# Norm shifts moved from GpSimd to VectorE, C rows asked for three places behind B rows, and a rewritten order table

## The chip, the cores and the metric

The kernel runs on one core of one Trainium2 chip. TensorE (PE), VectorE (DVE), ScalarE (ACT) and GpSimd (POOL) each run their own instruction list in order and wait for each other by semaphores. SyncE (SP) issues most of the transfers. The metric is device time of one launch, in microseconds. The kernel before took 2023.14 us in the median of three runs (2008.57, 2023.14 and 3804.73 us).

## The reference

Eight sequences of 512 tokens with 256 features go through four layers: an attention without a softmax over the score matrix (layer 0), two state-space layers (1 and 2, the second on permuted tokens), and another attention (layer 3). Every layer starts with a norm over the features, and the attentions have a second norm behind their products. Cut to what matters here:

```python
xn = (x - mean) * rsqrt(var + 1e-5)                        # "norm": root = rsqrt, shift = -mean * root
# state-space layer: 512 channels, 16 states each
xz = modulated(xn) @ W_in;  u = silu(conv4(xz[:512]));  z = xz[512:]
dt_r, B, C = split(u @ W_x, [64, 80]);  dt = softplus(dt_r @ W_dt + b_dt)
for t in range(512):                                       # h: [512 channels, 16 states]
    h = h * exp(dt[t, :, None] * A) + (dt[t] * u[t])[:, None] * B[t]
    y[t] = h @ C[t]
out = x + gate * (((y + u * D) * silu(z)) @ W_out)
```

## The kernel before

A **scan** is one state-space layer of one sequence; there are 16 of them. Channels lie on the 128 partitions in 4 chunks, tokens on the free axis. One **unit** is the recurrence of one chunk and one of the 16 states over all 512 tokens: one scan instruction of VectorE (lines 1578 and 1581). A scan has 64 units, the program 1024. Two units that follow each other share a state number, so that they share a row of B and a row of C: there are 512 such pairs, called rows below.

For a pair the work goes like this. SP asks for the row of B and the row of C from DRAM, spread over the partitions (lines 893 and 897; each has 4 slots). The **injection** is `dt*u*B`: for pairs of one kind ("beside", 224 of them) POOL makes it in the state buffer (line 960), for the others ("spread", 288) ACT copies the row of B into a PSUM bank (line 1292) and VectorE multiplies there (line 1571). ACT makes the decay `exp(dt*A)`, in a PSUM bank (line 1284) or in SBUF (line 1303). VectorE scans. Then the **weight**, the state times C, is made by POOL in place (line 969; VectorE does the last two pairs), and PE adds the weighted states up in PSUM (line 2016), which frees the state buffer. There are 14 state buffers of one unit each.

Beside the units run chains of other work: 16 attentions, and for every scan a prep (norm, projections, convolution), a tail and a post. Each is a generator with named stages. A norm that ACT makes is: sums, squares, `root` (Ln and Exp, lines 1015 and 1017), then POOL's **shift** (line 919, 128 x 4 elements, one instruction), then four `normed` activations on ACT that read the shift (line 1042). Five attention norms and one prep norm are made by VectorE instead; their `normed` (line 1428) doesn't read the shift, but the shift is still made, since its semaphore counts norms. There are 48 shifts: 32 of attentions and 16 of preps.

What sets the order: nothing at run time. `run_batches` walks through all units in quarter-unit steps, and each engine, building its own list, issues in each step what the tables say: `STEPS` (how many quarter units before or behind its scan an injection, a row copy, a decay, a weight or a sum stands), `GATES`, `SKIPS`, and the `*_STAGES` tables with the step of each stage of each chain. So the tables are the order of all engines' lists, and a wait at the head of a list holds all that stands behind it. 1024 units are 4096 quarter units.

SP's list, per scan, is: ask for B of row g as soon as its slot is free (`used`), then for C of row g-1 as soon as POOL's weight of the row four before it is done (`past(sp, m_prod, ...)`), then B of row g+1, and so on.

Of the kernel before, what the change touches and what calls it, by code (L numbers as in the profile page):

```python
# [17 lines left out]
HALVES = 2  # L18
# [12 lines left out]
TAIL_BASE, POST_BASE, PREP_BASE = -19, -50, 8  # L31
ATT_BASES, LATE_BASES = (18, 100, 153, 222), (41, 193)
# [11 lines left out]
LATE_PAIRS = 2  # L44
PIECES = 3
# [32 lines left out]
def by_name(names, durations):  # L78
# [146 lines left out]
         225),  # L225
})
TAIL_STAGES = by_name(TAIL_NAMES, {
    0: (104, 105, 106, 106, 109),
    1: (2, 68, 72, 73, 75),
    2: (61, 75, 78, 86, 91),  # L230
    3: (59, 73, 77, 85, 91),
# [1882 lines left out]
```

## Time and profile before

| | |
|---|---|
| runs | 2008.57, 2023.14, 3804.73 us |
| the profiled execution | 2021.5 us, span 2019.3 us |
| granted TensorE clock, mean of the span | 0.961 |
| busy, of the span | PE 90%, DVE 88%, ACT 85% (1710.2 us), POOL 89% |
| first and last work of POOL on a scan | 108.15 us, 1957 us |
| first and last scan instruction of VectorE | 113.56 us, 1957.84 us |

The busy shares alone don't separate the engines: four are near 90% of the span. The span has three parts: 108 us in which the weights and masks are loaded and the first attentions and the first prep run, 1849.7 us from POOL's first instruction for a scan to VectorE's last scan, and 61.5 us for the last post and the last attention, which run one behind the other.

### The profile page before, as it was taken

The page shows a single profiled execution, that of the slowest core. Times are in us where ns is not written, and L with a number is a line of the kernel's source. Part 1 is how long each engine was busy: PE and PEld are TensorE (multiplying, and loading weights), DVE is VectorE, ACT ScalarE, POOL GpSimd, SP SyncE. Part 2 cuts the span into 40 slices and gives each one's busy share as a digit, 9 for nine tenths or more (in the row PEclk, how much of TensorE's full clock was granted, in tenths as well). Part 3 has the DMA queues.
Part 4 walks back from the last instruction along what each step waited for, and adds up shares of the span by engine and source line. Part 5 has one row for each costly group of instructions (what it writes and reads, how often), then busy time and mean ns, then how long its engine had stood idle before and what let it go on. Part 6 is the DMA issues. An engine that isn't in the chain of part 4 may idle for free. (4 is left out here: it accounts for less than half of the span.)

```text
span 2019.3 us, 29111 instructions
## 1 busy us (share of the span) xinstructions
PE 1817.7 (90%) x9252; PEld 1265.7 (63%) x9252; DVE 1780.9 (88%) x1818; ACT 1710.2 (85%) x3224; POOL 1789.5 (89%) x823
## 2 busy tenths in 40 slices
PE   8979688998989999998999999898998999697778
PEld 7555555757667575766667575656757575455666
DVE  5458999889999999999989999999989999898983
ACT  2488788989989999999989999999989998777662
POOL 0059999999999999999999999999999999999970
PEclk8989699999999999999999999999999999898999
DMA  7034554444445545454444545445444545454430
GB/s 279 1 110 156 169 165 149 139 159 155 150 140 171 167 146 181 130 182 153 146 150 152 178 149 175 147 157 162 157 140 155 166 154 180 142 162 142 155 105 11
DMA packets 163784, 302.29 MB, mean 150 GB/s; under 512 B 18904, under 2 KB 27312, under 8 KB 162096
## 3 DMA queue, kind: packets, MB, share of 16 engines
q1 hardware_dynamic: 153110, 287.45, 43.9%
q10 hardware_dynamic: 10522, 12.99, 2.1%
q8 instruction: 74, 1.21, 0.2%
q14 instruction: 78, 0.64, 0.1%
HBM read 292.98 MB, written 5.29 MB: 148 GB/s over the span
## 5 line engine op out<-in xcount | busy, mean ns | idle before, releaser
L969 POOL TENSOR_TENSOR state<-state,c_rows 128x1024 f32<-128x1024 f32 x510 | 1197.2, 2382 | 26.3 <-DVE state L1578 13.6
L1581 DVE TENSOR_TENSOR_SCAN state<-decay,mix_banks 128x512 f32<-128x512 f32 x576 | 673.1, 1206 | 15.7 <-ACT decay L1303 0.7
L2016 PE MATMUL bank<-const_sb,state 128*128 128x128 f32 x4096 | 546.4, 281 | 38.1 <-POOL state L969 37.7
L2016 PEld LDWEIGHTS bank<-const_sb,state 128*128 128x128 f32 x4096 | 482.1, 145 | 145.9 <-issue 76.4
L1578 DVE TENSOR_TENSOR_SCAN state<-mix_banks,state 128x512 f32<-128x512 f32 x448 | 525.4, 1204 | 48.0 <-ACT mix_banks L1284 36.4
L960 POOL TENSOR_TENSOR state<-kept,b_rows 128x1024 f32<-128x1024 f32 x224 | 532.4, 2381 | 19.7 <-DMA b_rows<-flat_rows 10.3
L1303 ACT ACTIVATE decay<-kept,ssm_pack 128x512 f32<-128x512 f32 x576 | 395.2, 716 | 17.0 <-DVE state L1581 14.2
L1571 DVE TENSOR_TENSOR mix_banks<-kept,mix_banks 128x1024 f32<-128x1024 f32 x288 | 353.5, 1227 | 42.4 <-ACT mix_banks L1292 33.6
L1284 ACT ACTIVATE mix_banks<-kept,ssm_pack 128x512 f32<-128x512 f32 x448 | 302.0, 683 | 57.4 <-DVE state L1581 42.2
L1836 PE MATMUL bank<-kept,conv_diag 128*128 128x512 f32 x496 | 225.3, 597 | 4.3 <-ACT kept L1224 3.8
L987 ACT ACT_TABLE_LOAD x165 | 211.7, 1283 | 8.8 <-issue 5.8
L1698 PE MATMUL bank<-att_pack,xnT 128*128 128x256 f32 x704 | 187.5, 409 | 0.0
L1292 ACT ACTIVATE mix_banks<-b_rows 128x512 f32<-128x512 f32 x288 | 169.2, 589 | 21.4 <-DVE state L1578 16.9
L1698 PEld LDWEIGHTS bank<-att_pack,xnT 128*128 128x128 f32 x704 | 131.0, 197 | 38.3 <-issue 23.3
L1836 PEld LDWEIGHTS bank<-kept,conv_diag 128*128 128x128 f32 x496 | 90.8, 191 | 97.4 <-issue 90.6
L935 POOL TENSOR_TENSOR kept<-kept 128x1024 f32<-128x1024 f32 x32 | 76.1, 2378 | 53.1 <-ACT kept L1161 49.7
L1825 PE MATMUL bank<-ssm_pack,kept 128*128 128x512 f32 x256 | 117.6, 596 | 3.9 <-ACT kept L1215 1.9
L1815 PE MATMUL bank<-kept,ssm_pack 128*128 128x512 f32 x256 | 118.0, 597 | 0.7 <-ACT kept L1203 0.4
L1905 PE MATMUL bank<-gated_w,kept 128*128 128x256 f32 x480 | 108.0, 381 | 2.6 <-ACT kept L1268 2.4
L1905 PEld LDWEIGHTS bank<-gated_w,kept 128*128 128x128 f32 x480 | 89.5, 190 | 16.4 <-issue 5.0
L919 POOL TENSOR_TENSOR att_shift<-att_minus,att_rstd 128x4 f32<-128x4 f32 x32 | 6.7, 209 | 98.5 <-ACT att_rstd L1017 98.5
L1677 PE MATMUL bank<-const_sb,xn 128*128 128x128 f32 x352 | 56.9, 286 | 26.9 <-ACT xnT L1144 10.5
(206 smaller groups left out, 2237.9 us busy)
## 6 DMA issues: line engine op xcount, KB each, us to landing
b_rows<-flat_rows SPq DMA_DIRECT2D x512, 256.0 KB, 3.9
c_rows<-flat_rows SPq DMA_DIRECT2D x512, 256.0 KB, 3.6
conv_diag<-conv_diag SPq DMA_DIRECT2D x8, 1024.0 KB, 7.3
out<-x_res ACTq DMA_DIRECT2D x8, 512.0 KB, 3.2
ssm_pack<-ssm_pack SPq DMA_DIRECT2D x2, 1907.0 KB, 12.4
x_next<-x ACTq DMA_DIRECT2D x6, 512.0 KB, 6.7
x_again<-x_dbl ACTq DMA_DIRECT2D x16, 128.0 KB, 4.3
state<-ada_w SPq DMA_DIRECT2D x1, 1536.0 KB, 14.3
```

The costliest lines, as they stand in the source:

```text
L960: pool.tensor_tensor(pair_states(g), dtu[:, c:c + HC], by_pair(b_rows[:, row % ROWS]), ALU.mult).then_inc(m_inject[BESIDE], 1)
L969: pool.tensor_tensor(st, st, by_pair(c_rows[:, row % ROWS]), ALU.mult).then_inc(m_prod, 1)
L987: act.preload_act_table_set(name)
L1284: act.activation(mix_banks[BANK_OF[g]], dt[:, c, :], ACT.Exp, scale=neg_a[scan_of(si)[0]][:, c * N + n:c * N + n + 1]).then_inc(m_decay[BE ...
L1303: act.activation(decay[:, nth(g) % DECAYS, :], dt[:, c, :], ACT.Exp, scale=neg_a[scan_of(si)[0]][:, c * N + n:c * N + n + 1]).then_inc(m_d ...
L1571: dve.tensor_tensor(both, dtu[:, c:c + HC, :], by_pair(mix_banks[row]), ALU.mult).then_inc(m_inject[SPREAD], 1)
L1578: ins = dve.tensor_tensor_scan(st, mixed, st, 0.0, ALU.mult, ALU.add)
L1581: ins = dve.tensor_tensor_scan(st, decay[:, nth(g) % DECAYS], mixed, 0.0, ALU.mult, ALU.add)
L1698: ins = pe.matmul(dst, lhs[:, c, t * P:(t + 1) * P], weights[:, c, :], start=False, stop=(t % 2 == 1 and c == DC - 1))
L1836: ins = pe.matmul(dst[:, late:], conv_diag[:, c * TAPS + TAPS - 1 - late, :], u[s][:, c, 0:T - late], start=(late == 0), stop=(late == TAP ...
L1905: ins = pe.matmul(dst[:, (t % 2) * D:(t % 2 + 1) * D], lhs[:, c, t * P:(t + 1) * P], weights[:, c, :], start=(c == 0), stop=(c == CH - 1))
L2016: ins = pe.matmul(y_banks[c2][:, t * P:(t + 1) * P], state[:, g % STATES, t * P:(t + 1) * P], ident, start=False, stop=(g == BANK_SUMS[g / ...
```

## The change

Three things change. The shift goes from POOL's list to VectorE's, with the same operands and the same semaphores (for norms that VectorE makes itself, it stands ahead of `normed`). C rows are asked for three places behind their B rows, not one. And all tables of the order are new: the two that place POOL's work stand, in the mean, at 13.0 quarter units behind the scan for a weight (12.0 before) and 16.8 ahead of it for an injection (15.2 before); the sums stand 24.9 behind (24.5 before).

```diff
-TAIL_BASE, POST_BASE, PREP_BASE = -19, -50, 8
-ATT_BASES, LATE_BASES = (18, 100, 153, 222), (41, 193)
+TAIL_BASE, POST_BASE, PREP_BASE = -17, -46, 9
+ATT_BASES, LATE_BASES = (18, 100, 152, 221), (41, 193)
...
+C_BEHIND = 3
...
 STEPS = {
-    "weight": (11, 7, 10, 5, 9, 8, 6, 8, 9, 14, 14, 11, 15, 13, 12, 8, 7, 8, 12, 7, 5, 8, 6, 12, 11, 19, 17, 14,
...
+    "weight": (9, 5, 8, 8, 9, 8, 6, 15, 11, 10, 10, 14, 13, 9, 9, 6, 7, 7, 10, 6, 7, 8, 6, 16, 13, 13, 13, 10, 9,
...
-                for g in range(HALVES * N + 1):
+                for g in range(HALVES * N + C_BEHIND):
...
-                    if g > 0:
-                        slot, n = (g - 1) % ROWS, (g - 1) % N
-                        past(sp, m_prod, si * HALVES * N + g - ROWS)
+                    if g >= C_BEHIND:
+                        g -= C_BEHIND
+                        slot, n = g % ROWS, g % N
+                        past(sp, m_prod, si * HALVES * N + g + 1 - ROWS)
                         sp.dma_start(c_rows[:, slot, :], flat_rows[parity, N + n].partition_broadcast(P)).then_inc(c_loaded[slot], 16)
...
-            def shift(norm, root, done, k):
-                pool.wait_ge(root, k)
-                pool.tensor_tensor(norm["shift"][:, :, 0], norm["minus"][:, :, 0], norm["rstd"][:, :, 0],
-                                   ALU.mult).then_inc(done, 1)
...
             def attention(ai, layer, s, b):
-                w = Walk(ATT_STAGES[ai])
-                yield from w.to("root")
-                shift(att_norm, a_root, a_rstd, 2 * ai + 1)
-                yield from w.to("yroot")
-                shift(att_norm, a_root, a_rstd, 2 * ai + 2)
+                yield from ()
...
+            def shift(norm, root, done, k):
+                dve.wait_ge(root, k)
+                dve.tensor_tensor(norm["shift"][:, :, 0], norm["minus"][:, :, 0], norm["rstd"][:, :, 0],
+                                  ALU.mult).then_inc(done, 1)
...
+                yield from w.to("root")
+                shift(att_norm, a_root, a_rstd, 2 * ai + 1)
                 yield from w.to("xn")
...
+                yield from w.to("yroot")
+                shift(att_norm, a_root, a_rstd, 2 * ai + 2)
+                if (ai, 1) in VECTOR_NORMS:
                     yield from w.to("yn")
...
+                yield from w.to("root")
+                shift(prep_norm, p_root, p_rstd, pi + 1)
+                if pi in VECTOR_PREPS:
                     yield from w.to("xn")
```

The last shift of a prep (of scan 15, in the stretch near 1760 us of the profile before) stands on POOL like this before (L969 is a weight, L960 an injection):

```order
L969 TENSOR_TENSOR state<-state,c_rows 128x1024 x2
L960 TENSOR_TENSOR state<-kept,b_rows 128x1024
L919 TENSOR_TENSOR prep_shift<-prep_minus,prep_rstd 128x4
L969 TENSOR_TENSOR state<-state,c_rows 128x1024 x2
L960 TENSOR_TENSOR state<-kept,b_rows 128x1024
```

In the changed kernel POOL's list has weights, injections and 32 products of dt and u, and no shift. The same shift stands on VectorE like this (L1585 and L1582 are scans, L1575 the injection in PSUM):

```order
L1556 TENSOR_TENSOR x_res<-bank,x_next 128x512 x2
L1585 SCALAR_TENSOR_TENSOR state<-decay,mix_banks 128x512
L1582 SCALAR_TENSOR_TENSOR state<-mix_banks,state 128x512 x2
L1575 TENSOR_TENSOR mix_banks<-kept,mix_banks 128x1024
L1418 TENSOR_TENSOR prep_shift<-prep_minus,prep_rstd 128x4
L1585 SCALAR_TENSOR_TENSOR state<-decay,mix_banks 128x512 x2
L1582 SCALAR_TENSOR_TENSOR state<-mix_banks,state 128x512 x2
```

All scans behind it in VectorE's list now stand behind its wait for ACT's root.

SP's list at the start of a scan is this before (L893 asks for a row of B, L897 for a row of C):

```order
L893 DMA b_rows<-flat_rows 128x512 x2
L897 DMA c_rows<-flat_rows 128x512
L893 DMA b_rows<-flat_rows 128x512
L897 DMA c_rows<-flat_rows 128x512
L893 DMA b_rows<-flat_rows 128x512
```

and in the changed kernel (L894 is B, L899 is C):

```order
L894 DMA b_rows<-flat_rows 128x512 x4
L899 DMA c_rows<-flat_rows 128x512
L894 DMA b_rows<-flat_rows 128x512
L899 DMA c_rows<-flat_rows 128x512
L894 DMA b_rows<-flat_rows 128x512
```

Four rows of B now stand ahead of the first row of C, and the request for B of row r stands behind that for C of row r-4, which waits for the weight of row r-8; before it stood behind C of row r-2, which waits for the weight of row r-6.

## Rows read from the trace of the kernel before

**Rows 1.** The page: the span, and busy time of each engine (share) xinstructions.

```profile
span 2019.3 us, 29111 instructions
...
PE 1817.7 (90%) x9252; PEld 1265.7 (63%) x9252; DVE 1780.9 (88%) x1818; ACT 1710.2 (85%) x3224; POOL 1789.5 (89%) x823
```

**Rows 2.** Busy time by stretch; columns as its first line says.

```profile
core 0: us, PE busy (x) PEld busy (x) DVE busy (x) ACT busy (x) POOL busy (x), PEclk, DMA share, GB/s
0.00:108.15 108.15, 101.09 (x489) 71.88 (x490) 54.93 (x155) 38.98 (x67) 2.94 (x13) 0.91 0.36 133
...
108.15:1957.84 1849.69, 1664.40 (x8454) 1152.10 (x8453) 1704.37 (x1614) 1657.47 (x3131) 1786.18 (x808) 0.96 0.48 155
...
1957.84:2019.30 61.46, 52.22 (x311) 41.73 (x309) 21.62 (x50) 13.75 (x27) 0.40 (x2) 1.00 0.05 18
...
1500.00:1957.84 457.84, 385.08 (x2020) 275.30 (x2020) 427.80 (x401) 379.20 (x694) 450.71 (x202) 0.95 0.48 153
```

**Rows 3.** Groups of POOL, 108.5 to 1957.8 us: busy, mean ns | idle before, releasers.

```profile
L969 POOL TENSOR_TENSOR state<-state,c_rows 128x1024 f32<-128x1024 f32 x510 | 1197.2, 2382 | 26.3 <-DVE state L1578 13.6 <-DVE state L1581 12.3
L960 POOL TENSOR_TENSOR state<-kept,b_rows 128x1024 f32<-128x1024 f32 x224 | 532.4, 2381 | 19.7 <-DMA b_rows<-flat_rows 10.3 <-PE bank L2016 7.6 <-DVE state L1578 0.8
L935 POOL TENSOR_TENSOR kept<-kept 128x1024 f32<-128x1024 f32 x32 | 76.1, 2378 | 53.1 <-ACT kept L1161 49.7 <-issue 3.4
L919 POOL TENSOR_TENSOR att_shift<-att_minus,att_rstd 128x4 f32<-128x4 f32 x27 | 5.7, 211 | 6.8 <-ACT att_rstd L1017 6.8
L919 POOL TENSOR_TENSOR prep_shift<-prep_minus,prep_rstd 128x4 f32<-128x4 f32 x15 | 3.2, 216 | 1.1 <-ACT prep_rstd L1017 1.1
```

**Rows 4.** POOL's waits, 143 to 1957.8 us: total, times, longest.

```profile
POOL state L969 <- DVE state L1578: 13.6, 13, 2.2
POOL state L969 <- DVE state L1581: 12.3, 14, 2.2
...
POOL state L960 <- DMA b_rows<-flat_rows: 5.2, 9, 1.7
```

**Rows 5.** Timeline of POOL: start, duration, instruction [idle before].

```profile
147.41 0.20 POOL L919 TENSOR_TENSOR prep_shift<-prep_minus,prep_rstd 128x4 f32<-128x4 f32 x1
147.56 4.67 POOL L969 TENSOR_TENSOR state<-state,c_rows 128x1024 f32<-128x1024 f32 x2
...
172.21 9.32 POOL L969 TENSOR_TENSOR state<-state,c_rows 128x1024 f32<-128x1024 f32 x4
181.49 2.37 POOL L960 TENSOR_TENSOR state<-kept,b_rows 128x1024 f32<-128x1024 f32 x1
```

**Rows 6.** Groups of VectorE, whole span: two of the loop and two small instructions.

```profile
L1578 DVE TENSOR_TENSOR_SCAN state<-mix_banks,state 128x512 f32<-128x512 f32 x448 | 525.4, 1204 | 48.0 <-ACT mix_banks L1284 36.4 <-POOL state L960 10.3
L1571 DVE TENSOR_TENSOR mix_banks<-kept,mix_banks 128x1024 f32<-128x1024 f32 x288 | 353.5, 1227 | 42.4 <-ACT mix_banks L1292 33.6
...
L1380 DVE TENSOR_TENSOR mod_all<-mod_all,mod_raw 128x8 f32<-128x8 f32 x8 | 1.4, 178 | 0.3
...
L1423 DVE TENSOR_SCALAR att_minus<-att_mean_var 128x4 f32<-128x4 f32 x5 | 0.8, 163 | 0.0
```

**Rows 7.** Timeline of VectorE at the places of two shifts.

```profile
117.77 2.33 DVE L1578 TENSOR_TENSOR_SCAN state<-mix_banks,state 128x512 f32<-128x512 f32 x2
...
1757.81 1.23 DVE L1571 TENSOR_TENSOR mix_banks<-kept,mix_banks 128x1024 f32<-128x1024 f32 x1
```

**Rows 8.** Timeline of ACT: the roots that these two shifts read.

```profile
122.69 0.21 ACT L1017 ACTIVATE att_rstd<-att_var_eps 128x4 f32<-128x4 f32 x1
...
1760.24 0.20 ACT L1017 ACTIVATE prep_rstd<-prep_var_eps 128x4 f32<-128x4 f32 x1
```

**Rows 9.** SP's longest wait: total, times, longest.

```profile
SPq L897 <- POOL state L969: 1372.6, 506, 8.8
```

**Rows 10.** Transfers: count, KB each, median us from issue to landing.

```profile
b_rows<-flat_rows SPq DMA_DIRECT2D x512, 256.0 KB, 3.9
c_rows<-flat_rows SPq DMA_DIRECT2D x512, 256.0 KB, 3.6
```

More of the change, by code:

```diff
@@ L198 @@
-    2: (199, 199, 210, 213, 215, 217, 219, 218, 218, 218, 224, 230, 231, 237, 240, 246, 251, 254, 257, 265, 269,
-        273, 276),
-    3: (216, 216, 218, 218, 219, 221, 222, 224, 224, 224, 226, 228, 230, 232, 237, 239, 245, 251, 253, 255, 258,
-        264, 266),
-    4: (201, 201, 206, 211, 216, 215, 217, 216, 216, 216, 218, 219, 219, 221, 228, 234, 237, 240, 240, 240, 240,
-        240, 240),
-    5: (213, 213, 216, 216, 218, 217, 221, 220, 220, 220, 224, 222, 227, 229, 234, 238, 240, 242, 242, 242, 242,
-        242, 242),
@@ L206 @@
-    6: (203, 203, 206, 210, 215, 220, 221, 222, 222, 222, 224, 227, 231, 233, 245, 251, 254, 261, 265, 268, 271,
-        274, 274),
-    7: (213, 213, 216, 216, 218, 219, 223, 222, 222, 222, 226, 225, 228, 230, 237, 240, 246, 253, 255, 260, 264,
-        267, 274),
-    8: (201, 201, 210, 213, 214, 215, 217, 216, 216, 216, 218, 218, 220, 222, 228, 234, 237, 240, 240, 240, 240,
-        240, 240),
-    9: (204, 204, 206, 212, 216, 217, 219, 218, 218, 218, 220, 219, 223, 225, 231, 236, 239, 246, 246, 246, 246,
-        246, 246),
@@ L222 @@
-    14: (202, 202, 210, 211, 212, 215, 216, 218, 218, 218, 218, 218, 219, 220, 226, 229, 231, 230, 237, 239, 245,
-         252, 254),
-    15: (3, 3, 144, 144, 145, 147, 147, 154, 172, 206, 207, 207, 208, 210, 213, 213, 217, 214, 217, 221, 224, 224,
-         225),
+    0: (181, 181, 182, 183, 183, 190, 193, 200, 200, 200, 203, 201, 204, 206, 213, 219, 221, 224, 224, 224, 224,
+        224, 224),
+    1: (189, 189, 190, 197, 202, 202, 203, 203, 203, 203, 204, 204, 207, 209, 216, 220, 223, 226, 226, 226, 226,
+        226, 226),
@@ new lines @@
+    2: (183, 183, 198, 199, 201, 202, 211, 203, 203, 203, 215, 215, 220, 221, 224, 232, 234, 237, 240, 248, 253,
+        257, 260),
+    3: (200, 200, 203, 202, 203, 205, 206, 206, 206, 206, 209, 209, 214, 215, 220, 223, 228, 238, 239, 244, 251,
+        254, 256),
+    4: (184, 184, 186, 193, 197, 199, 201, 200, 200, 200, 202, 201, 203, 205, 211, 217, 221, 224, 224, 224, 224,
+        224, 224),
+    5: (195, 195, 198, 199, 201, 202, 202, 202, 202, 202, 203, 204, 205, 208, 214, 220, 222, 226, 226, 226, 226,
+        226, 226),
@@ new lines @@
+    6: (187, 187, 194, 196, 199, 205, 206, 207, 207, 207, 209, 213, 215, 217, 229, 236, 238, 243, 248, 252, 254,
+        256, 258),
+    7: (197, 197, 202, 202, 202, 204, 207, 206, 206, 206, 209, 210, 214, 217, 221, 224, 230, 238, 239, 245, 250,
+        252, 256),
+    8: (185, 185, 190, 197, 198, 199, 201, 200, 200, 200, 202, 202, 203, 205, 211, 217, 221, 224, 224, 224, 224,
+        224, 224),
+    9: (189, 189, 194, 197, 198, 201, 203, 202, 202, 202, 204, 205, 207, 209, 215, 220, 223, 230, 230, 230, 230,
+        230, 230),
@@ new lines @@
+    10: (187, 187, 194, 198, 202, 203, 213, 204, 204, 204, 215, 215, 221, 222, 228, 234, 238, 243, 249, 252, 255,
+         258, 260),
+    11: (198, 198, 200, 199, 200, 203, 204, 204, 204, 204, 206, 208, 210, 215, 220, 222, 228, 236, 238, 242, 253,
+         253, 256),
+    12: (187, 187, 194, 196, 197, 200, 201, 201, 201, 201, 202, 202, 203, 205, 211, 217, 221, 224, 224, 224, 224,
+         224, 224),
+    13: (187, 187, 190, 192, 196, 198, 199, 202, 202, 202, 202, 203, 203, 205, 211, 217, 223, 226, 226, 226, 226,
+         226, 226),
@@ L226 @@
+    14: (185, 185, 190, 192, 198, 202, 203, 207, 207, 207, 209, 208, 211, 213, 219, 222, 226, 230, 236, 239, 244,
+         250, 254),
+    15: (1, 1, 74, 114, 125, 129, 130, 131, 143, 190, 191, 191, 192, 194, 197, 197, 201, 198, 201, 205, 208, 208,
+         209),
 })
 TAIL_STAGES = by_name(TAIL_NAMES, {
[L228 to L231, printed above, removed]
-    4: (73, 88, 91, 93, 95),
-    5: (62, 75, 77, 79, 86),
-    6: (61, 75, 76, 79, 88),
@@ L235 @@
-    7: (61, 75, 77, 80, 92),
-    8: (74, 88, 89, 90, 94),
-    9: (63, 75, 77, 81, 89),
-    10: (62, 75, 77, 81, 90),
-    11: (62, 75, 76, 84, 91),
-    12: (69, 88, 90, 91, 94),
-    13: (62, 75, 76, 77, 89),
-    14: (56, 75, 80, 83, 89),
-    15: (59, 74, 77, 82, 87),
+    0: (96, 97, 98, 98, 101),
+    1: (0, 61, 65, 66, 67),
+    2: (55, 67, 70, 72, 83),
+    3: (62, 65, 67, 80, 84),
+    4: (66, 81, 83, 85, 87),
+    5: (64, 67, 68, 77, 82),
+    6: (53, 67, 69, 75, 82),
+    7: (53, 67, 69, 74, 83),
@@ L244 @@
+    8: (66, 79, 82, 83, 87),
+    9: (64, 67, 68, 74, 81),
+    10: (53, 68, 73, 75, 82),
+    11: (51, 67, 69, 77, 83),
+    12: (61, 80, 82, 83, 85),
+    13: (64, 67, 73, 76, 82),
+    14: (47, 66, 70, 74, 80),
+    15: (48, 65, 68, 80, 84),
 })
-SETUP_STAGES = dict(zip(SETUP_NAMES, (2, 47, 25, 51, 62, 96, 80, 84, 121, 147, 73, 168, 176, 179), strict=True))
+SETUP_STAGES = dict(zip(SETUP_NAMES, (2, 47, 25, 56, 77, 96, 80, 84, 121, 147, 73, 168, 176, 179), strict=True))
 ALL_UNITS = SCANS * UNITS
@@ L249 @@
 STEPS = {
-    "bank": (5, 7, 1, 5, 2, 5, 9, 3, 8, 8, 8, 8, 9, 4, 9, 5, 3, 5, 10, 8, 10, 7, 8, 8, 7, 8, 10, 8, 8, 7, 8, 8, 11,
[14 rows of a table removed]
-    "row": (6, 2, 7, 8, 7, 5, 11, 8, 8, 6, 8, 12, 3, 4, 8, 10, 8, 8, 2, 7, 12, 8, 7, 3, 11, 7, 6, 8, 8, 11, 6, 8,
[8 rows of a table removed]
-    "beside": (11, 9, 19, 21, 24, 27, 36, 37, 2, 3, 13, 8, 10, 12, 32, 34, 18, 19, 30, 33, 44, 24, 27, 29, 34, 37,
[22 rows of a table removed]
-    "inject": (14, 28, 29, 27, 19, 18, 14, 3, 19, 27, 24, 17, 14, 11, 10, 10, 11, 12, 16, 19, 4, 10, 10, 12, 10,
[8 rows of a table removed]
-    "weight": (11, 7, 10, 5, 9, 8, 6, 8, 9, 14, 14, 11, 15, 13, 12, 8, 7, 8, 12, 7, 5, 8, 6, 12, 11, 19, 17, 14,
[18 rows of a table removed]
@@ L325 @@
-    "sum": (31, 30, 27, 23, 20, 17, 13, 10, 15, 14, 13, 14, 15, 12, 30, 28, 25, 23, 35, 32, 28, 25, 22, 18, 30, 27,
[39 rows of a table removed]
-}
-GATES = (7, 14, 18, 18, 20, 22, 19, 19, 26, 26, 16, 18, 16, 18, 18, 19, 16, 18, 16, 18, 18, 22, 18, 22, 26, 30, 18, 18, 14, 18, 14, 15, 16, 18, 16, 16, 18, 34, 18, 20, 22, 34, 16, 18, 14, 18, 16, 19, 16, 18, 16, 18, 26, 38, 20, 20, 20, 26, 18, 18, 14, 16, 4, 5)
-SKIPS = (29, 32, 19, 21, 20, 43, 26, 35, 19, 25, 27, 36, 19, 21, 17, 19, 17, 19, 17, 19, 18, 42, 24, 34, 21, 46, 32, 35, 19, 25, 18, 19, 15, 17, 17, 19, 16, 42, 32, 36, 22, 48, 34, 36, 19, 30, 17, 19, 16, 20, 18, 19, 16, 43, 35, 39, 22, 45, 25, 33, 19, 36, 15, 16)
+    "bank": (7, 8, 1, 4, 9, 2, 7, 4, 8, 8, 8, 8, 9, 4, 10, 8, 3, 5, 4, 4, 1, 3, 8, 8, 7, 8, 10, 6, 4, 5, 8, 8, 11,
[13 rows of a table added]
@@ new lines @@
+    "row": (6, 9, 7, 4, 7, 6, 8, 8, 8, 3, 10, 13, 7, 6, 5, 10, 8, 8, 2, 4, 10, 8, 7, 4, 10, 8, 4, 7, 6, 9, 5, 8, 8,
[8 rows of a table added]
+    "beside": (11, 9, 19, 22, 24, 25, 35, 13, 2, 5, 4, 7, 9, 12, 30, 33, 18, 19, 30, 33, 44, 26, 27, 29, 2, 5, 16,
[22 rows of a table added]
+    "inject": (13, 28, 34, 27, 29, 29, 23, 4, 20, 29, 29, 25, 27, 10, 9, 16, 13, 10, 13, 14, 18, 23, 13, 22, 9, 11,
[8 rows of a table added]
+    "weight": (9, 5, 8, 8, 9, 8, 6, 15, 11, 10, 10, 14, 13, 9, 9, 6, 7, 7, 10, 6, 7, 8, 6, 16, 13, 13, 13, 10, 9,
[19 rows of a table added]
+    "sum": (31, 30, 27, 23, 20, 17, 13, 10, 17, 14, 13, 10, 13, 12, 24, 22, 19, 17, 35, 32, 28, 25, 22, 18, 34, 31,
[39 rows of a table added]
+}
@@ new lines @@
+GATES = (10, 16, 16, 18, 26, 38, 18, 20, 26, 34, 16, 18, 16, 18, 16, 20, 14, 16, 16, 18, 18, 26, 18, 18, 26, 38, 18, 22, 14, 16, 14, 14, 16, 18, 16, 18, 18, 20, 18, 20, 30, 34, 16, 18, 16, 18, 16, 18, 14, 16, 16, 18, 20, 30, 18, 18, 18, 18, 22, 22, 30, 40, 4, 5)
+SKIPS = (29, 32, 20, 23, 17, 39, 39, 42, 18, 42, 29, 39, 18, 26, 17, 19, 18, 19, 16, 18, 16, 39, 20, 34, 19, 21, 31, 40, 19, 38, 16, 18, 17, 18, 17, 19, 19, 44, 25, 35, 22, 48, 36, 38, 19, 30, 17, 19, 15, 18, 16, 18, 16, 39, 32, 38, 19, 38, 18, 25, 24, 28, 34, 45)
@@ L938, in before @@
                 w = Walk(PREP_STAGES[pi])
-                yield from w.to("root")
-                shift(prep_norm, p_root, p_rstd, pi + 1)
                 yield from w.to("mul")
```

12 lines of the change are left out of this document (removed), and 426 rows, old and new, of tables (ATT_STAGES, PREP_STAGES, STEPS).

## The prediction, on record before the change was run

> **What bounds the kernel now.** I read the busy shares first, to see that they don't decide: four engines stand between 85% and 90% of the span [rows 1]. Then the stretches. POOL has next to nothing to do in the first 108.15 us and in the last 61.46 us; in the 1849.69 us between, it is busy for 1786.18, 96.6%, against 92.1% for VectorE (1704.37) and 90% for TensorE and ACT [rows 2]. So in the stretch that makes up 92% of the span POOL is the nearest to a bound, with 63.5 us idle, and VectorE is the next, with 145.3 us idle. In the last 457.84 us of the stretch POOL idles for 7.1 us only [rows 2]; what can still be won there is POOL's own work.
>
> POOL's work in the stretch is 510 weights, 224 injections, 32 products of dt and u, and 42 of the 48 shifts (27 and 15) [rows 3]. The first 766 start 2.32 us apart when nothing holds them (181.49 less 172.21, over four) [rows 5], 1777 us in all. The other 73 us of the stretch are what a change could win at most while POOL does these 766: shifts, and waits. The waits are in the same rows: 26.3 us ahead of weights, nearly all for VectorE's scans, 19.7 ahead of injections, some 8 ahead of the shifts, and a few at the products (most of the 53.1 us there is the start itself) [rows 3].
>
> **The change, step by step.** The sum is made against the profiled execution, 2021.5 us, of which 2.2 us lie outside the span. The median of the three runs, 2023.14, is 0.1% above it.
>
> *Shifts leave POOL.* Each takes 0.15 us from its start to that of the next instruction (147.41 to 147.56) [rows 5]; 42 make 6.3 us of pure POOL time. POOL also stood idle ahead of them until ACT's root was there: 6.8 and 1.1 us, 7.9 together [rows 3]. Nothing covers either, since POOL's next weight stood behind them in the list: 14.2 us less, the one gain that the rows show whole.
>
> *Shifts come to VectorE.* An instruction of this size takes 0.163 us there (128x4, one input) or 0.178 (128x8, two inputs) [rows 6]: I take 0.17, so 42 cost 7.1 us. VectorE now waits for ACT's root too. I held the new places against the trace: the shift behind the fourth scan finds VectorE done at 120.10 and the root at 122.90, a wait of 2.8 us; the one in the order rows of the last prep finds 1759.04 and 1760.44, a wait of 1.4 us [rows 7, 8]. These are the first and the last of 11 such places among the 42; together they make 7.7 us if nothing else moved, about what POOL waited. So VectorE loses 14.8 us of its 145.3 idle. Queued behind a waiting shift are scans; behind them POOL's weights and ACT's decays that need a bank. A delay reaches POOL only where a weight stands close behind its scan. That happened at 27 of 510 weights [rows 3, 4], but VectorE's own idle time also comes from a loop with ACT (36.4 us for decays in banks, 33.6 for row copies [rows 6]), where a delay isn't simply caught up. I pass on a third, 5 us; the ends are 0 and 14.8.
>
> What could be dearer here is that the shift reads both inputs from SBUF while POOL reads SBUF nearly all the time. No VectorE instruction of the loop does that: each of those in rows 6 with mix_banks has one input in PSUM. So the price beside a running POOL isn't in the trace. Its ends are 0.17 us, and 0.17 plus one whole POOL instruction of 2.38 [rows 3]. I take the low end, as the nearest row by size (0.178, two SBUF inputs, with POOL idle) [rows 6], and keep the other as a rival. The Trainium skill, "SBUF — State Buffer", section "Who interferes with whom", speaks against this change: it says that a VectorE instruction with two SBUF inputs contends with a GpSimd instruction that reads SBUF, and that whoever starts first holds the shared ports to its end. By that rule the price would be half a POOL instruction in the mean, and the time that of the second rival; no row of this trace shows it.
>
> *C behind B.* SP spends 1372.6 us waiting for POOL's weights to free a slot of C [rows 9], and a row of B queues behind that. B of row r was asked for after the weight of row r-6, and is now after that of r-8, so B is no longer late where its own slot is free. POOL's waits for B after the start are nine, 5.2 us [rows 4]; I take half, 2.6. (Of the 10.3 in all [rows 3], 5.1 belong to the start, on which I count for nothing.) The request for C now also stands behind the wait for the slot of B three rows on. A row of the stretch lasts 3.61 us (1849.69 over 512), a C row is asked for when the weight four rows before it is done, thus about three rows, 10.8 us, ahead of need, and takes 3.6 us to land [rows 10]. The cover is 7 us, so I cost the later request at nothing; if the cover went, each of 510 weights could wait, and that would show at once.
>
> *The new tables.* A quarter unit is 0.45 us (1849.69 over 4096). The weights stand one quarter unit later behind their scans. The 27 waits for scans total 25.9 us [rows 4], 0.96 each; 0.45 less at each would be 12.2. A weight put later pushes what stands behind it, so I take half, 6; the ends are 25.9 less, and as much more, as nothing in an order's averages excludes new waits. Injections stand 0.7 us farther ahead, and need their state buffers that much sooner: the 7.6 us of waits for TensorE's sums [rows 3] may grow by some 4 us, or be left as they are; I take 0. The start and the end keep their lists but for six shifts that VectorE now makes ahead of its own norms: 6 times 0.17, 1 us more.
>
> Sum: -14.2 + 5 - 2.6 - 6 + 1 = -16.8, thus **2005 us** from 2021.5, 0.8% below. The ends of the terms alone: the largest gain, with all waits for scans and B rows gone and nothing passed on by VectorE, is 14.2 + 5.2 + 25.9 = 45 us (1976); the worst, with 25.9 us of new waits, 4 at the sums and all of VectorE's 14.8, is 31 us more (2052).
>
> **Rivals.**
>
> *Nothing is won.* POOL comes 14 us earlier to its weights and finds the scans not ready: the stretch is set by VectorE, ACT and POOL taking turns, and POOL's idle time only moves from the shifts to the weights. For it: VectorE waits 70 us for what ACT puts into banks (36.4 and 33.6) [rows 6], and a freer POOL shortens none of that. Against it: POOL is 98.4% busy in the last 457.84 us and VectorE isn't [rows 2]. Time: 2021.5, give or take 5.
>
> *The shift waits for POOL on VectorE.* A mechanism of two engines at one memory: the shift starts only when the POOL instruction that is running ends. POOL runs 96.6% of the stretch in pieces of 2.38 us, so the mean wait is half a piece, 1.19 us, and 42 make 50 us on VectorE, whose idle time falls from 145 to some 80 us. If half of that, and of the 14.8 us above, reaches the end, the time is 2005 + 25 + 2 = **2032 us**, slower than before; if a third does, as in my sum, 2005 + 17 = 2022; if all does, 2005 + 50 + 10 = 2065. It decides against the change from about a third on. For it: no row shows such a pair of inputs beside POOL that runs undelayed. Against it: VectorE has almost three times that idle time in the stretch [rows 2].
>
> *POOL runs through.* With the shifts gone, B rows early and weights later, POOL's remaining waits (63.5 less 7.9, 55.6 us) go for the most part, as they already have in the last 457.84 us. Two thirds gone is 37 us: 2021.5 - 14.2 - 37 = **1970 us**. For it: 7.1 us of idle time in that last piece [rows 2] shows that the order can do it. Against it: there fewer chains run beside the scans, and ACT is 83% busy (379.20 us), not 90% as over the stretch [rows 2].
>
> **How the numbers follow.** My forecast has 50%, from 1985 to 2016. Nothing won has 18%, the wait for POOL 20%, POOL running through 12%. The range for 8 in 10 reaches from 1982 to 2034: it takes in the forecast, nothing won, and the middle of the second rival, and leaves out the larger part of POOL running through and the upper end of the wait for POOL. About 2% is what a measurement of this kernel can tell from no change: below 1983 or above 2064. Faster by that takes most of POOL running through and an edge of the forecast, 10%; slower takes the upper end of the wait for POOL and of the new waits, 4%; the rest, 86%, is within.
>
> **What would show it.** POOL's list in the stretch has no idle time ahead of small instructions, and its busy time falls by some 7 us; waits for B rows after the start are below 3 us; no wait of a weight for a C row appears. On VectorE the mean of the 48 shifts decides the second rival: near 0.17 us for my sum, above 1 us for the rival (or as much idle time ahead of them that is put down to nothing). POOL's waits for scans should be below 25.9 us; if they have grown by 14 us or more, nothing was won. My forecast is wrong if waits that the trace didn't show before, at a state buffer, a C row or a bank, come to more than 10 us.

## The result, and the profile after

The changed kernel takes 2050.11 us in the median of four runs (2040.67 to 2051.9), the kernel before, on the same chip, 2020.12 us; the ratio is 1.0158, with a 95% interval from 1.0099 to 1.0218. The 2020.12 is the median of four runs of which one, of 3804.73 us, was a slow one that the ratio leaves out. So the changed kernel is slower by 1.6%, where I had forecast 0.8% faster and a range that ended at 2034 us. The profiled execution took 2049.57 us.

Busy time of each engine in the changed kernel, which answers [rows 1], first for the whole span and then by the three stretches of [rows 2], with the columns of that group:

```profile
span 2047.6 us, 29108 instructions
...
PE 1816.4 (89%) x9252; PEld 1264.4 (62%) x9252; DVE 1850.8 (90%) x1866; ACT 1713.2 (84%) x3224; POOL 1783.3 (87%) x775
```

```profile
0.00:107.09 107.09, 99.74 (x490) 70.34 (x491) 55.34 (x159) 39.70 (x68) 2.15 (x9) 0.92 0.37 134
107.09:1986.00 1878.91, 1665.13 (x8462) 1153.24 (x8462) 1773.89 (x1656) 1659.70 (x3130) 1781.18 (x766) 0.96 0.49 153
1986.00:2047.60 61.60, 51.56 (x303) 40.78 (x301) 21.55 (x52) 13.78 (x27) 0.00 (x0) 0.99 0.05 18
```

The start and the end are as long as before. The stretch of the scans is 29.2 us longer (1849.69 to 1878.91). POOL lost 5.0 us of work there, as the shifts left it, but its idle time rose from 63.5 to 97.7 us. VectorE works 69.5 us more (1704.37 to 1773.89), 48 instructions of four columns (42 of them in the stretch) being all that was added to its list. Its costliest groups, which answer [rows 6] (busy time, mean ns of one | idle time before them and what ended it):

```profile
L1585 DVE TENSOR_TENSOR_SCAN state<-decay,mix_banks 128x512 f32<-128x512 f32 x576 | 673.8, 1206 | 17.0 <-ACT decay L1294 3.2
L1582 DVE TENSOR_TENSOR_SCAN state<-mix_banks,state 128x512 f32<-128x512 f32 x448 | 523.9, 1203 | 29.5 <-ACT mix_banks L1275 25.3 <-POOL state L951 3.8
L1575 DVE TENSOR_TENSOR mix_banks<-kept,mix_banks 128x1024 f32<-128x1024 f32 x288 | 353.4, 1227 | 25.6 <-ACT mix_banks L1283 16.6
L1418 DVE TENSOR_TENSOR att_shift<-att_minus,att_rstd 128x4 f32<-128x4 f32 x32 | 43.3, 1355 | 5.3 <-ACT att_rstd L1008 5.2
...
L1418 DVE TENSOR_TENSOR prep_shift<-prep_minus,prep_rstd 128x4 f32<-128x4 f32 x16 | 34.5, 2158 | 0.9 <-ACT prep_rstd L1008 0.3
```

A shift takes 1.36 us in the mean in the attentions and 2.16 in the preps, together 77.8 us for 48, where I had put 0.17 each. Scans and injections take what they took. Six shifts lie outside the stretch and take 0.15 or 0.16 us each, so the 42 inside take 76.8 us, 1.83 each. The wait for ACT's root, which I had put at 7.7 us, is 6.2.

What a long one looks like: VectorE, POOL and ACT around the shift at 288.56 us (start, duration, instruction, idle time before it).

```profile
287.42 1.23 DVE L1575 TENSOR_TENSOR mix_banks<-kept,mix_banks 128x1024 f32<-128x1024 f32 x1
288.56 6.72 DVE L1418 TENSOR_TENSOR att_shift<-att_minus,att_rstd 128x4 f32<-128x4 f32 x1
295.20 2.32 DVE L1585 TENSOR_TENSOR_SCAN state<-decay,mix_banks 128x512 f32<-128x512 f32 x2
```

```profile
288.30 6.96 POOL L960 TENSOR_TENSOR state<-state,c_rows 128x1024 f32<-128x1024 f32 x3
297.66 2.35 POOL L960 TENSOR_TENSOR state<-state,c_rows 128x1024 f32<-128x1024 f32 x1 [2.41 <-DVE state L1585]
```

```profile
295.31 1.09 ACT L1033 ACTIVATE xn<-x_next,att_shift,att_rstd 128x256 f32<-128x256 f32 x2 [6.17 <-DVE att_shift L1418]
```

The shift begins 0.26 us after a weight of POOL has begun, and ends at 295.28, when POOL's third weight in a row ends (288.30 + 6.96 = 295.26). ACT's `normed` then starts, 6.17 us late. And POOL, whose next weight needs the scan that stood behind the shift, stands still for 2.41 us. The other shifts of the stretch read the same way: each of the 42 ends within 0.06 us of the end of a POOL instruction. In 35 it is the instruction that was running, and they take 1.08 us in the mean; seven outlast two to four of POOL's instructions (2.72 to 7.83 us, 39.0 us together), and each of these seven ends where POOL then idles for 1.29 to 4.13 us for want of a scan.

Who waits for whom now (total us, times, longest), of POOL from 143 to 1986 us, which answers [rows 4], and of ACT over the whole span:

```profile
POOL state L960 <- DVE state L1585: 46.1, 39, 4.1
POOL state L960 <- DVE state L1582: 14.6, 18, 2.4
POOL state L951 <- PE bank L2020: 14.0, 15, 2.4
...
POOL state L951 <- DMA b_rows<-flat_rows: 2.5, 2, 1.8
```

```profile
ACT kept L1033 <- DVE prep_shift L1418: 26.9, 11, 7.9
...
ACT xn L1033 <- DVE att_shift L1418: 24.0, 14, 6.2
```

POOL's waits for scans were 25.9 us in 27 and are 60.7 in 57. ACT waits 50.9 us for shifts, in front of decays and row copies for VectorE. In the kernel before it waited 2.3 us for them:

```profile
ACT kept L1042 <- POOL prep_shift L919: 1.5, 2, 1.0
ACT xn L1042 <- POOL att_shift L919: 0.8, 1, 0.8
```

### The profile page after: what moved, and what is told of

Same layout as the page of the kernel before. It is cut to its first block and busy times, and to the rows that moved or that the text cites. A ratio compares the mean times of both kernels' runs of the same rounds, so it can differ in the third digit from the quotient of the medians.

```text
span 2047.6 us, 29108 instructions
## 1 busy us (share of the span) xinstructions
PE 1816.4 (89%) x9252; PEld 1264.4 (62%) x9252; DVE 1850.8 (90%) x1866; ACT 1713.2 (84%) x3224; POOL 1783.3 (87%) x775
## 5 line engine op out<-in xcount | busy, mean ns | idle before, releaser
L960 POOL TENSOR_TENSOR state<-state,c_rows 128x1024 f32<-128x1024 f32 x510 | 1195.5, 2369 | 68.6 <-DVE state L1585 51.3
L1585 DVE TENSOR_TENSOR_SCAN state<-decay,mix_banks 128x512 f32<-128x512 f32 x576 | 673.8, 1206 | 17.0 <-ACT decay L1294 3.2
L1582 DVE TENSOR_TENSOR_SCAN state<-mix_banks,state 128x512 f32<-128x512 f32 x448 | 523.9, 1203 | 29.5 <-ACT mix_banks L1275 25.3
L1575 DVE TENSOR_TENSOR mix_banks<-kept,mix_banks 128x1024 f32<-128x1024 f32 x288 | 353.4, 1227 | 25.6 <-ACT mix_banks L1283 16.6
L1829 PE MATMUL bank<-ssm_pack,kept 128*128 128x512 f32 x256 | 122.1, 618 | 5.8 <-ACT kept L1206 5.5
L1829 PEld LDWEIGHTS bank<-ssm_pack,kept 128*128 128x128 f32 x256 | 47.9, 199 | 54.6 <-issue 46.0
```

Of the source, the lines that this page charges most:

```text
L960: pool.tensor_tensor(st, st, by_pair(c_rows[:, row % ROWS]), ALU.mult).then_inc(m_prod, 1)
L1575: dve.tensor_tensor(both, dtu[:, c:c + HC, :], by_pair(mix_banks[row]), ALU.mult).then_inc(m_inject[SPREAD], 1)
L1582: ins = dve.tensor_tensor_scan(st, mixed, st, 0.0, ALU.mult, ALU.add)
L1585: ins = dve.tensor_tensor_scan(st, decay[:, nth(g) % DECAYS], mixed, 0.0, ALU.mult, ALU.add)
```

## The experiments

Each ratio is to the kernel before, run on the same chip, with its 95% interval. Three theories stood first. P: a shift on VectorE is held by POOL's instructions. T: the new tables, or the later request for C, cost the time. W: VectorE standing for ACT's root costs it.

### Shifts back on POOL, the rest of the change kept

```diff
...
+                pool.wait_ge(root, k)
+                pool.tensor_tensor(norm["shift"][:, :, 0], norm["minus"][:, :, 0], norm["rstd"][:, :, 0],
+                                   ALU.mult).then_inc(done, 1)
...
-                dve.wait_ge(root, k)
-                dve.tensor_tensor(norm["shift"][:, :, 0], norm["minus"][:, :, 0], norm["rstd"][:, :, 0],
-                                  ALU.mult).then_inc(done, 1)
...
```

> The changed kernel with the 48 shifts put back on POOL; new tables and the request for C three places behind B are kept. Theory P (a shift on VectorE is held as long as POOL's instructions run): VectorE loses the 70 us that the shifts took too much (77.8 us for 48, against 0.17 each), the shifts on POOL take 0.2 us each, VectorE is busy for 1775 to 1790 us, POOL's waits for scans fall from 65.9 to 20 to 35 us; time 2000 to 2020 us. Theory T (the new tables or the later request for C are to blame): 2040 to 2055 us, POOL's waits for scans stay at 55 us or more. Theory W (VectorE standing for ACT's root, with scans behind it, is to blame, not the price of the instruction): 2000 to 2020 us as by P, so this run doesn't tell W from P.

1.0033 [1.0015, 1.0051], 2020.01 us. VectorE is busy 1779.4 us, POOL's waits for scans are 31.1 us. Tables and C request together cost 0.3%, so they don't make the 1.6%: T falls as the main cause. But they win nothing either, which my terms for them had.

### The shift as four instructions with one tensor input

```diff
-                dve.tensor_tensor(norm["shift"][:, :, 0], norm["minus"][:, :, 0], norm["rstd"][:, :, 0],
-                                  ALU.mult).then_inc(done, 1)
+                for t in range(TT):
+                    ins = dve.tensor_scalar(norm["shift"][:, t, :], norm["minus"][:, t, :], norm["rstd"][:, t, 0:1], None, ALU.mult)
+                ins.then_inc(done, 1)
```

> The changed kernel, but each shift on VectorE is four instructions with one tensor input each (128x1, the root as a scalar per partition) in place of one with two tensor inputs. Same place in the list, same wait for ACT's root. Theory P: no piece of a shift is held; each takes 0.13 to 0.2 us, four 0.65, 48 shifts 31 us in place of 77.8; the time falls to 2010 to 2030 us. Theory W: the wait for the root is what it was, and the instructions take 23 us more than 48 short ones would: 2045 us or more. If the pieces too are held, the scalar's read is enough for it, and the mean of a piece is above 0.3 us.

0.9897 [0.9863, 0.9932], 1993.77 us: below the kernel before and below the changed one, further than P had it. The groups of the shift on VectorE:

```profile
L1419 DVE TENSOR_SCALAR att_shift<-att_minus,att_rstd 128x1 f32<-128x1 f32 x128 | 17.9, 201 | 5.3 <-ACT att_rstd L1008 5.1
...
L1419 DVE TENSOR_SCALAR prep_shift<-prep_minus,prep_rstd 128x1 f32<-128x1 f32 x64 | 9.1, 205 | 0.9 <-ACT prep_rstd L1008 0.3
```

None of 192 is held: the longest takes 0.216 us. The wait for the root is the same 6.2 us as in the changed kernel, so W falls.

```profile
span 1991.0 us, 29252 instructions
...
PE 1799.7 (90%) x9252; PEld 1252.8 (63%) x9252; DVE 1799.1 (90%) x2010; ACT 1708.9 (86%) x3224; POOL 1781.6 (89%) x775
```

VectorE is busy 51.7 us less than in the changed kernel. The span is 56.6 us shorter, but the two ran on different chips; by their ratios (0.9897 and 1.0158) the difference is 2.6%, some 53 us, give or take 14. Within that, what the shifts took too much went to the end whole.

### The kernel before with the shift on VectorE, in both forms

Old tables, C one place behind B; the body of the function is the one or the other of the two above.

```diff
+            def shift(norm, root, done, k):
+                dve.wait_ge(root, k)
...
+                yield from w.to("root")
+                shift(att_norm, a_root, a_rstd, 2 * ai + 1)
                 yield from w.to("xn")
```

One instruction with two tensor inputs:

> The kernel before with one thing changed: the 48 shifts on VectorE, as one instruction with two tensor inputs. Old tables, C one place behind B. Theory P: the mean of a shift is above 1 us, the longest ones 5 us or more; VectorE busy 50 to 80 us more than before; time 2030 to 2055 us (1.005 to 1.02 of before). Theory T: shifts may be long, but the time is that of before, 2015 to 2025 us, as VectorE's idle time takes them.

1.0249 [1.0211, 1.0287], 2064.02 us, more than either theory said.

```profile
L1416 DVE TENSOR_TENSOR att_shift<-att_minus,att_rstd 128x4 f32<-128x4 f32 x32 | 40.4, 1262 | 6.1 <-ACT att_rstd L1006 5.9
L1416 DVE TENSOR_TENSOR prep_shift<-prep_minus,prep_rstd 128x4 f32<-128x4 f32 x16 | 31.0, 1940 | 4.4 <-ACT prep_rstd L1006 4.2
```

Four instructions with one:

> The kernel before with the 48 shifts on VectorE, each as four instructions with one tensor input. Theory P: no piece is held (0.13 to 0.2 us each, 31 us in all on VectorE); time within 0.5% of before, 2012 to 2030 us, and below the run that has the shift as one instruction with two tensor inputs. Theory W: as slow as that one, 2035 us or more.

1.0072 [1.0046, 1.0097], 2024.76 us, each instruction of 0.20 us. So the hold is there without the new tables, and its price is 1.8% (1.0249 against 1.0072). What is left, 0.7%, lies outside the half per cent that I had allowed: on the old order the move loses even with an undelayed shift.

### The later request for C alone

```diff
...
-                    if g > 0:
-                        slot, n = (g - 1) % ROWS, (g - 1) % N
-                        past(sp, m_prod, si * HALVES * N + g - ROWS)
+                    if g >= C_BEHIND:
+                        g -= C_BEHIND
+                        slot, n = g % ROWS, g % N
+                        past(sp, m_prod, si * HALVES * N + g + 1 - ROWS)
```

> The kernel before with C rows asked for three places behind their B rows; nothing else is changed. By the prediction's term: POOL's waits for rows of B after the start fall from 5.2 to below 3 us, none for a row of C appears, 2.6 us less in time, so the ratio to before lies within 0.3% of 1. Theory T (the tables or this request cost the time): 1.005 or more, with waits of weights for C rows.

0.9959 [0.9942, 0.9976], 2003.28 us. It is a gain of 0.4%, some 8 us (5 to 12 by the interval), three times my term and outside the 0.3% that I had allowed. From 143 us on no wait for a row of B or C is left among POOL's in this run.

### 128 small instructions on the kernel before

One ahead of every eighth unit, its result read by nothing; with two tensor inputs in one run, with one in the other:

```diff
...
+                if part == 0 and is_unit(g) and g % 8 == 4:
+                    dve.wait_ge(s_eps, 2)
+                    dve.tensor_tensor(spare[:, :, 0], att_norm["eps"][:, :, 0], prep_norm["eps"][:, :, 0], ALU.mult)
```

```diff
...
+                    dve.tensor_scalar(spare[:, :, 0], att_norm["eps"][:, :, 0], -1.0, None, ALU.mult)
```

> The kernel before with 128 more instructions on VectorE, one ahead of every eighth unit: 128x4, two tensor inputs in SBUF, into a tile that nothing reads, and with nothing to wait for. Theory P: each is held to the end of a POOL instruction or longer, mean 1.2 us or more, VectorE busy at least 150 us more, time 2110 us or more. Theory W (waiting for ACT's root is what cost the time): 128 times 0.17 is 22 us on VectorE, time 2010 to 2030 us.

> The same 128 instructions at the same places, with one tensor input in SBUF in place of two (128x4 times a constant). Theory P: none is held, 0.17 us each, 22 us on VectorE, time 2010 to 2030 us. If any VectorE instruction that keeps to SBUF is held by POOL, whatever the number of its inputs, this run is as slow as its twin with two inputs.

1.0665 [1.0619, 1.0711] and 1.0661 [1.0629, 1.0693]. The group of each, the first from the run with two inputs, the second from the one with one:

```profile
L1608 DVE TENSOR_TENSOR spare<-att_eps,prep_eps 128x4 f32<-128x4 f32 x128 | 183.7, 1435 | 0.5
```

```profile
L1608 DVE TENSOR_SCALAR spare<-att_eps 128x4 f32<-128x4 f32 x128 | 189.6, 1481 | 0.6
```

Nothing waits here, so W is out as the cause. But P falls too in the form that I had given it: with one tensor input the instruction is held as long. Yet the shift in four pieces, also with one tensor input, wasn't. So it isn't the number of tensors alone.

### Eight forms side by side

```diff
...
+                    form = (g // 8 + g // 64) % 8
+                    if form == 0:
+                        dve.tensor_scalar(spare[:, 0:1, 0], a[:, 0:1], -1.0, None, ALU.mult)
+                    elif form == 1:
+                        dve.tensor_tensor(spare[:, 0:1, 0], a[:, 0:1], b[:, 0:1], ALU.mult)
...
+                    elif form == 6:
+                        dve.tensor_scalar(spare[:, :, 0], a, b[:, 0:1], None, ALU.mult)
+                    elif form == 7:
+                        dve.reciprocal(spare[:, :, 0], a)
```

> The kernel before with 128 more instructions on VectorE at the same places as in the two runs with one form, but of eight forms in turn, 16 of each, all from SBUF to SBUF. Theory P as it stood (two tensor inputs in SBUF are what is held) fell with the one-input twin, which was held as much. Theory P2: held is what reads SBUF twice at a time, that is two tensor inputs, or one input of several elements that VectorE reads by halves (a multiplication by a constant); one element by a constant isn't, nor a reciprocal, of which the loop of the kernel before has some that run undelayed. P2 expects means of 0.13 to 0.2 us for one element by a constant and for the reciprocal, and 1 us or more for two tensors of 1, 3 and 4 elements and for four elements by a constant; three elements by a constant, and four by a scalar per partition, are open. Theory S (size alone: one element is never held): two tensors of one element run in 0.2 us too, and the reciprocal of four is held. The time lies between 2060 and 2130 us by either.

1.0573 [1.0533, 1.0613], 2132.18 us, 2 us above the range that both theories gave. The forms (count: shortest/median/longest in ns, first and last start):

```profile
L1611 DVE TENSOR_SCALAR spare<-att_eps x16: 126/128/145, 116.8 to 1958.1; 128x1 f32<-128x1 f32 x16
L1613 DVE TENSOR_TENSOR spare<-att_eps,prep_eps x16: 133/2114/6332, 141.1 to 1973.3; 128x1 f32<-128x1 f32 x16
L1615 DVE TENSOR_SCALAR spare<-att_eps x16: 143/1334/5418, 155.1 to 1986.2; 128x3 f32<-128x3 f32 x16
L1617 DVE TENSOR_TENSOR spare<-att_eps,prep_eps x16: 138/926/5504, 167.3 to 2005.0; 128x3 f32<-128x3 f32 x16
L1619 DVE TENSOR_SCALAR spare<-att_eps x16: 143/912/4871, 182.6 to 2021.4; 128x4 f32<-128x4 f32 x16
L1621 DVE TENSOR_TENSOR spare<-att_eps,prep_eps x16: 310/1200/5590, 198.4 to 2037.5; 128x4 f32<-128x4 f32 x16
L1623 DVE TENSOR_SCALAR spare<-att_eps,prep_eps x16: 204/833/5517, 212.3 to 2048.1; 128x4 f32<-128x4 f32 x16
L1625 DVE RECIPROCAL spare<-att_eps x16: 149/152/178, 223.3 to 1940.3; 128x4 f32<-128x4 f32 x16
```

Read the medians: two forms are never held, one element by a constant (128 ns) and the reciprocal (152 ns), all 32 beside a running POOL instruction. The other six have medians from 0.8 to 2.1 us and means from 1.15 to 2.77; seven of their 96 instructions fell into a pause of POOL, and those took 0.13 to 0.22 us. One element of two tensors is held, so P2 holds and S falls. The two open forms, three elements by a constant and four by a scalar per partition, are held.

### The two-input shift in four pieces

```diff
-                    ins = dve.tensor_scalar(norm["shift"][:, t, :], norm["minus"][:, t, :], norm["rstd"][:, t, 0:1], None, ALU.mult)
+                    ins = dve.tensor_tensor(norm["shift"][:, t, :], norm["minus"][:, t, :], norm["rstd"][:, t, :], ALU.mult)
```

> The changed kernel with each shift as four instructions of 128x1 with two tensor inputs: the same number of instructions, of elements, and the same waits as the run with one tensor input and a scalar per partition (1994 us), and only the second operand is read another way. Theory P2: each instruction can be held; mean of one above 0.5 us, VectorE busy for 1870 us or more, time 2045 us or more. Theory S: as the run with a scalar per partition, 1985 to 2005 us.

1.0492 [1.0465, 1.0518], 2111.5 us. Against the run with a scalar per partition, reading the root as a tensor and not as a scalar costs 118 us:

```profile
L1419 DVE TENSOR_TENSOR att_shift<-att_minus,att_rstd 128x1 f32<-128x1 f32 x128 | 89.3, 757 | 5.3 <-ACT att_rstd L1008 5.1
L1419 DVE TENSOR_TENSOR prep_shift<-prep_minus,prep_rstd 128x1 f32<-128x1 f32 x64 | 50.3, 845 | 0.8 <-ACT prep_rstd L1008 0.3
```

The shifts take 139.6 us in place of 27.0, 112.6 more, and the span is 117.0 us longer. Here too the delay reaches the end whole.

### The tables, told apart

The new tables with shifts on POOL and C one place behind B:

```diff
-C_BEHIND = 3
+C_BEHIND = 1
```

> The new tables alone: shifts on POOL, C rows asked for one place behind B as before. Against the run with shifts on POOL and C three places behind (1.0033 of before) it tells what the later request is worth in the new order: by the old order's 0.4%, 1.005 to 1.01 of before; if the new order doesn't need it, 1.000 to 1.005.

1.038 [1.0352, 1.0408], 2089.97 us: a miss of both guesses. The longest of POOL's waits, 143 to 2060 us:

```profile
POOL state L962 <- DMA b_rows<-flat_rows: 61.5, 38, 4.2
```

With C three places behind this wait is 1.5 us. That fits the new order, which puts injections farther ahead of their scans and so needs rows of B sooner than the old request order gives them. Last, the old tables with the request and the undelayed shift:

```diff
+C_BEHIND = 3
...
+                for t in range(TT):
+                    ins = dve.tensor_scalar(norm["shift"][:, t, :], norm["minus"][:, t, :], norm["rstd"][:, t, 0:1], None, ALU.mult)
...
```

> The kernel before (old tables) with the later request for C and with the shifts on VectorE as four one-input instructions: all of the changed kernel but its tables, without the hold. Against the run with the same shifts and the new tables (0.9897 of before) it is the worth of the tables once shifts aren't held. If the parts add up on the old tables (shifts so made 1.0072, the request 0.9959), it is 1.003, and the new tables are worth 1.3%, some 27 us. If the old tables profit from both, 0.985 to 0.995, and the new tables are worth nothing.

1.0029 [1.0006, 1.0052], as the sum of the parts. So with all else equal and no hold the new tables are worth 1.3% (0.9897 against 1.0029). With shifts on POOL they cost 0.7% (1.0033 against 0.9959). ACT's waits point at a reason. With the new tables it stands 35.0 us for shifts that POOL makes:

```profile
ACT kept L1044 <- POOL prep_shift L921: 21.0, 13, 3.1
...
ACT xn L1044 <- POOL att_shift L921: 14.0, 11, 2.9
```

With the old tables and the later request these waits are 2.3 us, and with the new tables and undelayed shifts on VectorE 6.7. No run shows that they are what makes the 0.7%.

### The shift on ACT

```diff
...
+                act.wait_ge(root, k)
+                for t in range(TT):
+                    ins = act.activation(norm["shift"][:, t, :], norm["minus"][:, t, :], ACT.Copy,
+                                         scale=norm["rstd"][:, t, 0:1])
+                ins.then_inc(done, 1)
...
```

> The changed kernel with the shift on ACT, as four instructions of 128x1 behind its own root; neither VectorE nor POOL makes shifts. By theory P VectorE loses all 77.8 us; ACT gets 48 times about 1 us, some 48 us, and needs no longer wait for VectorE ahead of `normed` (51 us in the changed kernel). If VectorE is what the new order hangs on: 1980 to 1995 us, at or below the run with four one-input instructions on VectorE (1994). If ACT's 48 us count as much as VectorE's: 2000 to 2020 us.

1.0022 [1.0004, 1.0041], 2017.45 us. VectorE falls to 1780.4 us, but 192 activations of 0.283 us put 40.8 us on ACT, and the time is as the second case said. The version with four one-input instructions on VectorE remains the best: 1.0% below the kernel before, 2.6% below the changed one by the two ratios.

## Why the prediction was wrong

**The step that failed is the price of a shift on VectorE**, in the term for the shifts that come to VectorE, +5. I set 0.17 us, the low end, "as the nearest row by size", from a row in which POOL was idle. What decided wasn't the size but what POOL does at that time, and 96.6% of the time it runs. Measured: 1.83 us in the stretch, 76.8 us for the 42 where I had 7.1. By the sign that the prediction had named, the mean of all 48 is 1.62 us, above the 1 us that spoke for the rival. Between the changed kernel and its twin with undelayed shifts that makes some 53 us of the time. The rival "the shift waits for POOL on VectorE" described it, at 50 us on VectorE; its mechanism is shown by the run with the shift in four pieces, by the same two forms on the old tables, by the two-input shift in four pieces and by the eight forms. It was too mild in two places.

*Half a POOL instruction in the mean.* That is right for 35 of the 42 (1.08 us). My upper end, a whole POOL instruction more (2.55 us), was exceeded by the other seven, which took half of the 76.8 us. The Trainium skill, "SBUF — State Buffer", section "Who interferes with whom", says that whoever starts first holds the shared ports for the whole instruction, and names besides two SBUF inputs also copies, casts and multiplications by a scalar, where they can use both port pairs. The eight forms agree: tensor times tensor is held at one, three and four elements, several elements by a scalar are, and the reciprocal, which isn't named there, runs free (0.15 us). The runs go further in the length: a waiting instruction of the changed kernel outlasted up to four POOL instructions, not one.

*A third passed on.* I argued from VectorE's 145.3 us of idle time. But the changed kernel and its undelayed twin differ by 51.7 us of VectorE's time and, by the two ratios, by some 53 us of the whole. Idle time in pieces between handshakes is no cover: the held shift stops scans, POOL runs dry behind them (60.7 us of waits for scans, 20.9 in the twin), and ACT stands before `normed` (50.9 us, 6.7 in the twin) with decays and row copies behind it. On the old tables a little is absorbed: with 128 held instructions VectorE is busy 164.4 us more (1945.3), and they cost 6.65%, 134 us.

**Shifts leave POOL, -14.2, and come to VectorE, +5.** POOL's list did nearly as forecast: 5.0 us less work in the stretch, where I had some 7, and its waits for roots gone. But on the old tables the undelayed shift on VectorE, in a form that costs 27 us there, is 0.7% slower, 14 us, not 9 us faster. My passing on of a third was too low here too; POOL's idle time moved to its waits for scans, as the rival "nothing is won" had it: with old tables and the later request they are 20.1 us with shifts on POOL and 41.8 with undelayed ones on VectorE.

**C behind B, -2.6.** Right in sign and in its tests: in the changed kernel the waits for B after the start are 2.5 us, and no weight waits for C. The size was low, 8 us on the old tables, where POOL's waits for B went whole (5.2 us) and those for scans fell as well, from 25.9 to 20.1. On the new ones it is a condition: without it, with shifts on POOL, they cost 3.8%.

**New tables, -6.** Not a term of its own. Worth +0.7% with shifts on POOL and -1.3% with undelayed shifts on VectorE. The waits at TensorE's sums, whose growth I set at 0, grew from 7.6 to 14.0 us in the changed kernel; in the twin with undelayed shifts they are 3.6, so the growth belongs to the hold and not to the tables.

With the hold taken away the change gives 0.9897, 2001 us from the profiled 2021.5, close to the 2005 that I had forecast. As the terms show, that is luck: it comes about by other amounts than mine. For its range the prediction needed a row of such an instruction beside a running POOL. There was none, and an unknown whose ends are 15 times apart should have had the middle of its rival, not its low end, as its value.

## What to carry over

Before moving a small instruction to VectorE beside a busy POOL, look at how it reads SBUF, not at how small it is: two tensors there, or several elements by a scalar, wait for POOL, and with them all that is queued behind. The longer POOL has run without a pause, the longer the wait can be. Write the instruction as one-element pieces by a scalar per partition, 0.20 us each here. An operand in PSUM may be another way: the scans and injections have one and ran at their usual time throughout (1.20 to 1.23 us), but no run tried it on a small instruction. A table of an order is worth something only together with the edits that it was made for, so take its parts away one by one before putting a price on any.

## What was not expected of the hardware

A waiting VectorE instruction isn't always served when POOL's running instruction ends. In the changed kernel it was passed over at 14 ends of POOL instructions and served at 37; one that had been passed over once was then served only where POOL stood still. On the old tables one lasted 9.67 us, to the fifth end. In the run with 128 two-input instructions 9 of the 11 that lasted longest ended ahead of a pause of POOL, and two ahead of POOL's own small shift. Since VectorE's delay is what makes POOL run dry, the hold ends itself.

Which ends let VectorE in goes with how long POOL has run without a pause. I counted it in six traces: the changed kernel, the two-input shift in four pieces, the two-input shift on the old tables, both runs with 128 instructions, and the six held of the eight forms. POOL's instructions are numbered from its last pause, which is any gap of 20 ns or more, and the ends taken are those at which POOL went on at once while VectorE had waited for 0.18 us or more. At the end of the first to the ninth instruction VectorE was served in all 296 cases, from the tenth on in 37 of 144. The shift at 288.56 came in POOL's fourteenth instruction since the pause before 258.18 (the second of the four in the last row), and was passed over at the ends of that and of the next:

```profile
258.18 2.35 POOL L960 TENSOR_TENSOR state<-state,c_rows 128x1024 f32<-128x1024 f32 x1 [0.66 <-DVE state L1585]
260.49 2.36 POOL L951 TENSOR_TENSOR state<-kept,b_rows 128x1024 f32<-128x1024 f32 x1
...
285.99 9.27 POOL L960 TENSOR_TENSOR state<-state,c_rows 128x1024 f32<-128x1024 f32 x4
```

What changes in POOL after some ten instructions, and why 37 of the later ends let VectorE in all the same, these traces don't tell.

One end of the changed kernel at which VectorE was served though POOL went on at once, in its second instruction since a pause: the shift starts at 734.54, POOL's injection ends at 736.54, POOL's weight follows without idle time, and the shift ends at 736.56.

```profile
734.54 2.02 DVE L1418 TENSOR_TENSOR prep_shift<-prep_minus,prep_rstd 128x4 f32<-128x4 f32 x1
```

```profile
731.87 2.37 POOL L960 TENSOR_TENSOR state<-state,c_rows 128x1024 f32<-128x1024 f32 x1 [0.35 <-DVE state L1585]
734.19 2.35 POOL L951 TENSOR_TENSOR state<-kept,b_rows 128x1024 f32<-128x1024 f32 x1
736.50 2.37 POOL L960 TENSOR_TENSOR state<-state,c_rows 128x1024 f32<-128x1024 f32 x1
```
